# Edge counts by blocks of 16 targets instead of 32, and the one-hots of a block made in two operations

## The reference

```python
xn = _layernorm(x)
neigh = jax.ops.segment_sum(xn[src], dst, num_segments=1250)      # 40,000 edges
rst = (1.0 + eps[0]) * xn + neigh
gnn = relu(rst @ W1 + b1) @ W2 + b2 + xn
attn = relu((q * SCALE) @ k.T) @ v                                # 8 heads of 64, over all 1250 rows
x = x + gnn + (attn @ W_out.T + b_out)
x = x + experts(_layernorm(x))                                    # 16 experts, the 2 best of each row
```

## Time and profile before

| | us |
|---|---|
| median of 3 runs | 813.71 |
| the profiled execution | 813.19 |
| its span | 811.4 |
| lay-out of the edges, up to the first projections' end | 26.0 to 65.6 |
| projections with counts | 65.6 to 123.8 |
| V projection with counts and sums | 123.8 to 168.0 |
| attention with counts and sums | 168.0 to 439.7 |
| output, dense layers, routing and experts | 439.7 to 811.4 |

### The profile page before, as it was taken

The page is one execution under the profiler, slowest core; times in us unless marked ns, Lnnn a source line. Parts: engine busy times, 40 slices in busy tenths (PEclk is TensorE's granted clock), DMA queues, the critical chain, the costliest instruction groups (busy, mean ns, idle before and its releaser), DMA issues.

```text
span 811.4 us, 11860 instructions
## 1 busy us (share of the span) xinstructions
PE 722.5 (89%) x3591; PEld 438.2 (54%) x3592; DVE 441.4 (54%) x1350; ACT 221.3 (27%) x456; POOL 133.8 (16%) x191
## 2 busy tenths in 40 slices
PE   4878889999999999999999999999995899999900
PEld 2444444455555555555555457778882367667600
DVE  5945665358788787697742233343556333332324
ACT  2212211133232232232332033233341033434400
POOL 8945334000000000000000000020212000000054
PEclk9899999999999999999999999999997589999955
DMA  9530000060634706173376500010238564343367
GB/s 293 164 130 0 1 0 2 0 241 35 259 113 161 266 10 260 74 253 135 140 271 228 213 0 1 1 64 15 79 133 321 239 250 137 105 138 121 116 186 233
DMA packets 48769, 109.34 MB, mean 135 GB/s; under 512 B 6700, under 2 KB 6716, under 8 KB 46272
## 3 DMA queue, kind: packets, MB, share of 16 engines
q1 hardware_dynamic: 43936, 89.03, 30.5%
q0 software_dynamic: 3616, 11.17, 4.4%
q10 hardware_dynamic: 1152, 8.39, 2.6%
HBM read 44.79 MB, written 63.78 MB: 134 GB/s over the span
## 4 chain that ended last, share of the span: by engine, by line
PE 81%; DVE 9%; POOL 3%; issue 3%; DMA 3%; ACT 1%; SPq 0%; POOLq 0%; DVEq 0%
PE bank L1208 11%; PE bank L1191 10%; PE bank L1299 8%; PE bank L1245 7%; PE bank L1360 7%; PE bank L1090 7%; PE bank L1127 6%; PE bank L1373 6%; PE bank L1159 5%; PE bank L1170 4%; PE bank L1230 4%; POOL arena L598 2%; PE bank L1336 2%; DMA arena<-in_x 2%; PE bank L1342 2%
## 5 line engine op out<-in xcount | busy, mean ns | idle before, releaser
L843 DVE TENSOR_SCALAR arena<-iota,arena 125x128 f16<-125x128 f16 x392 | 113.2, 289 | 43.8 <-PE bank L1090 32.5
L845 DVE TENSOR_SCALAR arena<-iota,arena 125x320 f16<-125x320 f16 x392 | 120.3, 307 | 0.0
L674 ACT ACTIVATE arena<-bank 128x416 f32<-128x416 f32 (+1 forms) x120 | 62.2, 518 | 155.1 <-PE bank L1191 152.1
L873 DVE TENSOR_SCALAR arena<-bank 128x416 f32<-128x416 f32 (+1 forms) x120 | 69.0, 591 | 61.8 <-PE bank L1191 61.6
L1208 PE MATMUL bank<-arena 128*64 128x416 f32 (+1 forms) x480 | 97.2, 525 | 0.4 <-DVE arena L873 0.4
L1159 PE MATMUL bank<-arena 128*128 128x416 f32 (+1 forms) x192 | 81.8, 579 | 3.2 <-DMA arena<-in_wqkv 1.9
L1090 PE MATMUL bank<-arena 125*128 125x320 f16 x392 | 72.1, 302 | 8.6 <-DVE arena L845 8.4
L1299 PE MATMUL bank<-arena 128*128 128x384 f32 (+2 forms) x256 | 70.3, 430 | 0.0
L1360 PEld LDWEIGHTS bank<-arena 128*128 128x128 f32 x448 | 52.8, 197 | 17.1 <-issue 15.7
L1360 PE MATMUL bank<-arena 128*128 128x128 f32 x448 | 55.1, 283 | 6.3 <-issue 5.3
L1159 PEld LDWEIGHTS bank<-arena 128*128 128x128 f32 x192 | 40.3, 217 | 35.5 <-issue 33.0
(11 more groups left out here) (210 smaller groups left out, 1033.3 us busy)
## 6 DMA issues: line engine op xcount, KB each, us to landing
slots<-arena SPq DMA_DIRECT2D x6, 5376.0 KB, 17.1
slots<-arena SPq DMA_DIRECT2D x2, 5120.0 KB, 16.6
arena<-in_ew SPq DMA_DIRECT2D x8, 1024.0 KB, 11.3
arena<-in_ew ACTq DMA_DIRECT2D x8, 1024.0 KB, 14.3
arena<-slots SPq DMA_DIRECT2D x32, 256.0 KB, 2.7
slots<-arena SPq DMA_DIRECT2D x28, 256.0 KB, 2.0
arena<-in_gw SPq DMA_DIRECT2D x2, 2048.0 KB, 10.2
arena<-in_wqkv SPq DMA_DIRECT2D x3, 1024.0 KB, 15.7
```

The costliest lines, as they stand in the source:

```text
L674: act.activation(probs[0:kt, s % NPB, 0, 0:n], bank[2 * (s % 2)][0:kt, 0:n], ACT.Relu).then_inc(p0_ready, 1)
L843: dve.tensor_scalar(ring[:, at_slot:at_slot + P], iota16[0:CE, 0:P], window_cols[:, i % WBUF, 1, k:k + 1], None, ALU.is_equal)
L845: dve.tensor_scalar(ring[:, at_slot + P:at_slot + OHW], iota16[0:CE, :], window_cols[:, i % WBUF, 0, k:k + 1], None, ALU.is_equal).then_in ...
L873: dve.tensor_single_scalar(probs[0:kt, s % NPB, 1, 0:n], bank[2 * (s % 2) + 1][0:kt, 0:n], 0.0, op=ALU.max).then_inc(p1_ready, 1)
```

## The change

- `WD` is 16: blocks of 16 targets, 80 of them. A block is given 6 chunks (the 79th 2, the last 1), 471 products in all, each 160 columns wide.
- DVE makes all one-hots of a block in two operations, `tensor_tensor` with both operands broadcast: the ramp over the chunks, the chunk's number over the ramp. One is 125 x 6 x 128, one 125 x 6 x 160. Before, each chunk had two `tensor_scalar` operations. The ring holds 2 blocks, and `onehots_ready` counts blocks.
- Two blocks stand side by side in a bank (`window_at`), and ACT copies both at once. The swap of two pairs at a change of windows is gone.
- POOL makes columns for 80 blocks of 6 instead of 40 of 10, into 8 places, four blocks ahead instead of two windows.
- `EARLY` is 16 and `EVERY` 1.675, so a stretch of targets has the same turns as before. A block is made in the turn of its first chunk; its products stand in the turns they would have by the old rule.
- The marks have 80 entries where they had 40, and are turned by two transposes in place of one.

```diff
-WD = 32
+WD = 16
-RING = 8
-WBUF = 4
+RING = 2
+WBUF = 8
+RW = max(-(-EDGES * WD // (N * CE)) + 1, 1) * OHW
...
+        def window_at(w):
+            return bank[AW[w // 2 % 2]][:, w % 2 * WCOL:w % 2 * WCOL + WCOL]
...
-        PREP, FROM, EARLY = 4, 8, 8
-        EVERY = 3.35
+        PREP, FROM, EARLY = 4, 8, 16
+        EVERY = 1.675
...
-                dve_after[made].append(("pair", w, k))
-                if w % 2 == 0 and k == USUAL[w] - 1:
-                    held = ("pair", w, k)
-                elif w % 2 == 1 and k == 0:
-                    pe_after[used(made)] += [("pair", w, k), held]
-                    act_after[used(made) + 1].append(("window", w - 1))
-                else:
-                    pe_after[used(made)].append(("pair", w, k))
+                if k == 0:
+                    dve_after[made].append(("window", w))
+                pe_after[used(made)].append(("pair", w, k))
             if w % 2 == 1:
-                act_after[used(made) + 1].append(("window", w))
+                act_after[used(made) + 1].append(("windows", w // 2))
...
-                    pool.wait_ge(onehots_ready, FIRST[w - WBUF + 1])
+                    pool.wait_ge(onehots_ready, w - WBUF + 1)
-            for _, what, i in sorted([(start(max(w - 2, 0)), "cols", w) for w in range(NW)]
+            for _, what, i in sorted([(start(max(w - 4, 0)), "cols", w) for w in range(NW)]
...
-                        act.activation(a_t[:, g % 2, :, (i % WPG) * WD:(i % WPG + 1) * WD],
-                                       bank[AW[i % 2]][:, 0:WCOL].rearrange("p (b d) -> p b d", b=NT),
+                        act.activation(a_t[:, g % 2, :, c:c + 2 * WD].rearrange("p b (a d) -> p b a d", a=2),
+                                       bank[AW[i % 2]][:, 0:2 * WCOL].rearrange("p (a b d) -> p b a d", a=2, b=NT),
...
-                if what == "pair":
-                    if k == 0:
-                        dve.wait_ge(cols_ready, i + 1)
-                    q = FIRST[i] + k
-                    if q >= RING:
-                        dve.wait_ge(onehots_used, q - RING + 2)
-                    dve.tensor_scalar(ring[:, at_slot:at_slot + P], iota16[0:CE, 0:P],
-                                      window_cols[:, i % WBUF, 1, k:k + 1], None, ALU.is_equal)
-                    dve.tensor_scalar(ring[:, at_slot + P:at_slot + OHW], iota16[0:CE, :],
-                                      window_cols[:, i % WBUF, 0, k:k + 1], None,
-                                      ALU.is_equal).then_inc(onehots_ready, 1)
+                if what == "window":
+                    n = USUAL[i]
+                    dve.wait_ge(cols_ready, i + 1)
+                    if i >= RING:
+                        dve.wait_ge(onehots_used, FIRST[i - RING + 1])
+                    hot = ring[:, i % RING * RW:i % RING * RW + n * OHW].rearrange("p (k c) -> p k c", c=OHW)
+                    for c, of in ((slice(0, P), 1), (slice(P, OHW), 0)):
+                        width = c.stop - c.start
+                        ins = dve.tensor_tensor(
+                            hot[:, :, c], iota16[0:CE, 0:width].unsqueeze(1).to_broadcast([CE, n, width]),
+                            window_cols[:, i % WBUF, of, 0:n].unsqueeze(2).to_broadcast([CE, n, width]), ALU.is_equal)
+                    ins.then_inc(onehots_ready, 1)
...
-                if k == 0 and w >= 2:
-                    pe.wait_ge(window_saved, w - 1)
-                q = FIRST[w] + k
-                pe.wait_ge(onehots_ready, q + 1)
-                product(w, ring, (q % RING) * OHW, k == 0, k == USUAL[w] - 1).then_inc(onehots_used, 1)
+                if k == 0 and w % 2 == 0 and w >= 4:
+                    pe.wait_ge(window_saved, w // 2 - 1)
+                if k == 0:
+                    pe.wait_ge(onehots_ready, w + 1)
+                product(w, ring, w % RING * RW + k * OHW, k == 0, k == USUAL[w] - 1).then_inc(onehots_used, 1)
```

More of the change, by code:

```diff
@@ L47 @@
 WCOL = NT * WD
-RING = 8
-WBUF = 4
+RING = 2
+WBUF = 8
 OHW = P + WCOL
-USUAL = [-(-EDGES * min(WD, N - w * WD) // (N * CE)) + 1 for w in range(NW)]
+RW = max(-(-EDGES * WD // (N * CE)) + 1, 1) * OHW
+USUAL = [-(-EDGES * max(0, min(WD, N - w * WD)) // (N * CE)) + 1 for w in range(NW)]
 FIRST = [sum(USUAL[:w]) for w in range(NW + 1)]
@@ L128, in layer @@
         marks = at(A_T + 2400, [2, NW, CJ], parts=CP)
-        marks2 = at(A_T + 3700, [2 * NW], parts=CP)
-        val_f = at(A_T + 4400, [500], parts=CP)
-        ring = at(RINGB, [RING * OHW // 2], parts=CE).bitcast(f16)
+        marks2 = at(A_T + 5000, [2 * NW], parts=CP)
+        val_f = at(A_T + 5700, [500], parts=CP)
+        ring = at(RINGB, [RING * RW // 2], parts=CE).bitcast(f16)
         src_i, dst_i, hi_i, lo_i, win_i, off_i = (
@@ L135, in layer @@
         NCP = NC + max(USUAL)
-        window_cols = at(RINGB + RING * OHW * 2, [WBUF, 2, max(USUAL)], parts=CE)
+        window_cols = at(RINGB + RING * RW * 2, [WBUF, 2, max(USUAL)], parts=CE)
         val = at(VALB, [NCP], parts=CE)
@@ L211, in layer @@
         last5 = sb("last5", [CP, CJ])
-        mincol = sb("mincol", [CP, 1])
+        mincol = sb("mincol", [NW, 2])
         minrow = sb("minrow", [1, 2 * NW])
@@ L620, in graph @@
                 for what, i in act_after[turn]:
[L621 to L624, removed]
+                    if what == "windows":
+                        act.wait_ge(onehots_used, FIRST[2 * i + 2])
+                        g, c = 2 * i // WPG, 2 * i % WPG * WD
+                        if c == 0 and g >= 2:
                             act.wait_ge(neigh_ps, g - 1)
-                        act.activation(a_t[:, g % 2, :, (i % WPG) * WD:(i % WPG + 1) * WD],
-                                       bank[AW[i % 2]][:, 0:WCOL].rearrange("p (b d) -> p b d", b=NT),
+                        act.activation(a_t[:, g % 2, :, c:c + 2 * WD].rearrange("p b (a d) -> p b a d", a=2),
+                                       bank[AW[i % 2]][:, 0:2 * WCOL].rearrange("p (a b d) -> p b a d", a=2, b=NT),
                                        copy).then_inc(window_saved, 1)
@@ L776, in _ @@
             dve.wait_ge(consts_ready, 2)
-            dve.tensor_single_scalar(win_i, dst_i, 5, op=ALU.arith_shift_right)
+            dve.tensor_single_scalar(win_i, dst_i, 4, op=ALU.arith_shift_right)
             dve.tensor_single_scalar(off_i, dst_i, WD - 1, op=ALU.bitwise_and)
@@ L803, in _ @@
             dve.wait_ge(mins_ps, 1)
-            dve.tensor_reduce(mincol[:, :], bank[AW[0]][0:2 * NW, 0:CP], X, ALU.min).then_inc(mincol_ready, 1)
+            dve.tensor_reduce(mincol[:, :], bank[AW[0]][0:NW, 0:2 * CP].rearrange("w (a p) -> w a p", a=2), X,
+                              ALU.min).then_inc(mincol_ready, 1)
             dve.wait_ge(min_ps, 1)
@@ L811, in _ @@
             link(dve.tensor_tensor(minrow[:, NW:2 * NW], minrow[:, NW:2 * NW], minrow[:, 0:NW], ALU.subtract))
-            for of, usual in ((minrow[:, NW:2 * NW - 1], USUAL[0]), (minrow[:, 2 * NW - 1:2 * NW], USUAL[NW - 1])):
+            full = N // WD
+            for of, usual in ((minrow[:, NW:NW + full], USUAL[0]), (minrow[:, NW + full:NW + full + 1], USUAL[full]),
+                              (minrow[:, NW + full + 1:2 * NW], USUAL[NW - 1])):
                 last = dve.tensor_scalar(of, of, float(1 - usual), 0.0, ALU.add, ALU.max)
@@ L834, in _, with do @@
             dve.sem_inc(chunks_ready, 1)
[L835 to L847 removed]
+            def do(what, i):
+                if what == "window":
[10 more added lines that the diff above has]
+                    ins.then_inc(onehots_ready, 1)
                 else:
@@ L1070, in lay_out_edges @@
                     pe.wait_ge(marks_ready, 1)
-                    pe.transpose(bank[AW[0]][0:2 * NW, 0:CP], marks2, ident[0:CP, 0:CP]).then_inc(mins_ps, 1)
+                    for a in range(2):
+                        ins = pe.transpose(bank[AW[0]][0:NW, a * CP:(a + 1) * CP], marks2[:, a * NW:(a + 1) * NW],
+                                           ident[0:CP, 0:CP])
+                    ins.then_inc(mins_ps, 1)
                 elif part == 1:
                     pe.wait_ge(mincol_ready, 1)
-                    pe.transpose(bank[NB][0:1, 0:CP], mincol[:, :], ident[0:CP, 0:CP]).then_inc(min_ps, 1)
+                    for a in range(2):
+                        ins = pe.transpose(bank[NB][0:1, a * NW:(a + 1) * NW], mincol[:, a:a + 1], ident[0:NW, 0:NW])
+                    ins.then_inc(min_ps, 1)
                 elif part == 2:
@@ L1118, in neighbours @@
                 if t == 0:
-                    pe.wait_ge(window_saved, WPG * (g + 1))
+                    pe.wait_ge(window_saved, WPG // 2 * (g + 1))
                     if g:
```

2 lines of the change are left out of this document (1 added, 1 removed).

## The result

| | median us | runs from to | profiled execution | its span |
|---|---|---|---|---|
| before | 813.43 | 812.87 to 814.99 | 813.19 | 811.4 |
| after | 819.81 | 819.24 to 820.42 | | 817.5 |

The change makes the kernel slower: the ratio is 1.0073, with a 95% interval of 1.006 to 1.0086. The prediction was 801, with a range of 790 to 812, and was wrong in the sign too. Nearly all of the miss lies in one stage.

The account below looks back on a forecast made before the run. TensorE was taken to bound attention and the V stage, with stalls in projection. Gains of 20.3 - 12 + 1.7 + 4.6 - 0.8 - 0.9 = 12.9 us took 813.19 to 800.3, median 801; range 790 to 812.

Parts of the forecast that it names:

- Count products: TensorE, three stages: 160-column products 0.072 us apart against 0.138 for 320; gain 20.3 us, 16.3 of it in attention.
- A block's 1.93 us of DVE: DVE's two one-hot operations for a block take 1.93 us with waits, bounds 1.75 and 2.5; DVE is not relieved.
- Lumps in attention, 12 us: Attention: one-hots made in lumps delay ReLUs and counts, so TensorE stalls 12 us in all; the least trusted term.
- The slope of 4 us for ten per cent: Attention: stalls grow by 4 us if a block takes 10% longer, and fall by 4 if 10% less.
- First episode, +1.7: Projection stage, block 3 beside POOL's split: 2.2 us stall, lower clock in half the cases, instead of 4.6; gain 1.7.
- Second episode, +4.6: Projection stage, 23.9 us after the first episode: block 7 is ready before its first product is due; no stall, gain 4.6.
- First block, -0.8: Projection stage: TensorE's first count waits for a block of 1.93 us rather than a pair, behind POOL's columns; loss 0.8.
- edge lay-out, -0.9: Projection stage, TensorE's wait for the marks: sixteen operations of 80 instead of 40 elements and a larger reduction; loss 0.9.
- "Nothing changes place on TensorE": TensorE, all stages: its part of the change taken as 471 products instead of 392, with a gain of 20.3 us.
- rival 1: Lumps eat the gain: a block takes 2.5 us, attention 10 more than before, the rest 6 less; 817 us, chance 0.10.

Follow-up runs that it names:

- single pairs: Changed kernel with the spread looks, attention's one-hots made chunk by chunk, each pair by two scalar-per-partition operations with its own count: 793.99 us, again 792.97.
- the spread looks: Changed kernel, each tile's four sequencer checks for surplus chunks (register load and branch) placed ahead of source blocks 3, 5, 7, 9, not all before the last: 802.62 us.
- two looks: Changed kernel with one sequencer check for surplus chunks (register load and branch) per four blocks instead of two, so two per 128-target tile: 803.03 us.
- the kernel before with four looks: Kernel before, with a sequencer check for surplus chunks per window of 32 targets instead of per two, so four per 128-target tile: 829.77 us, ratio 1.0185.

## Why the prediction was wrong, step by step

- **Count products**: the spacing is right, the sum 1.3 us too high. Seven take 0.59 us until the values begin; less the 0.09 for the change of kind, that is 0.071 each, where the sum had 0.072. But where a neighbour sum follows, the last count product costs 0.03 us at either width: three of 320 columns take 0.31 us until the sum begins, which is two spacings of 0.138 and 0.03, and four of 160 take 0.25, three spacings and 0.03. At these 19 places the narrower product saves nothing of the 0.066. With single pairs, where hardly a wait is left, attention is 13.1 us shorter than before; 16.3 less 1.3 and less the 1.7 of waits is 13.3. Timelines of TensorE, two rows of after and two of before:

```profile
213.94 0.66 PE L1097 MATMUL bank<-arena 125*128 125x160 f16 x7
214.53 1.62 PE L1215 MATMUL bank<-arena 128*64 128x416 f32 x8
...
248.61 0.58 PE L1090 MATMUL bank<-arena 125*128 125x320 f16 x3
248.92 0.51 PE L1127 MATMUL bank<-xn_hi,a_t 128*128 128x512 f32 x1
```

- **A block's 1.93 us of DVE**: right, 1.94. It did not get slower beside POOL's small operations; those get longer beside it (the subtraction up to 1.03 us instead of 0.24), which costs nothing.
- **Lumps in attention, 12 us**: right in mechanism and near in size. With the spread looks the waits for DVE come to 10.2 us, and making pairs singly again gives back 9.9 and leaves waits of 1.7. The longest one, at 305.54, is that of block 53, with a residual sum behind it, as the prediction said (2.3 forecast, 1.78 + 0.35 measured). The slope of 4 us for ten per cent was 3.2 at most.
- **First episode, +1.7**: better. The wait is 1.68 instead of 2.2, and no lower clock stands behind it, so some +2.9. **Second episode, +4.6**: gone, as forecast.
- **First block, -0.8, and edge lay-out, -0.9**: right and half of it. The projection behind the first block starts at 68.64 (the second row below, of after) instead of 67.36. Of these 1.28 us 0.48 come from the edge lay-out, as DVE begins at 66.05 instead of 65.57, and 0.8 from the block. What the forecast did not have: the lower clock behind this first wait lasts longer. The eight projections there take 5.42 us until the next count product (68.64 to 74.06), where they took 4.49 (67.36 to 71.85), 0.9 more. That the projection stage came out 6.9 us better against 7.1 is partly luck: the episode gave 1.2 more and the lay-out 0.4, the clock took 0.9, and the rest I did not trace.

```profile
68.13 0.72 PE L1097 MATMUL bank<-arena 125*128 125x160 f16 x4 [4.27 <-DVE arena L846]
68.64 3.75 PE L1166 MATMUL bank<-arena 128*128 128x416 f32 x5
```

- **"Nothing changes place on TensorE"**, and the sum that rested on it: this is the step that failed. The prediction's section on TensorE's counts took its part of the change to be 471 products instead of 392. It counted matrix instructions and waits, and left out what the sequencer executes between them: twenty more looks, two more in each row of two. They cost 17.4 us of attention (285.90 against 268.50 with the same looks spread), where the sum had nothing. None of the rivals had it either; rival 1 (817) came near the time for a reason that doesn't hold, as a block takes 1.94 and not 2.5 us. The trace of before had what was needed: the load of L1103 took 0.30 us at some tiles and 0.90 at three, two looks took some 3 us there, with no wait behind them. How much is queued ahead of such a row can be counted in the timeline (3.3 us, above), and then a third look would not have fitted; there were two more.

With that one thing taken away, by two looks or by spread ones, the kernel takes 803.0 or 802.6 us against a forecast of 801, and attention 268.5 to 268.9 against 267 to 268.

## What to carry to other kernels

When a change makes a loop's unit smaller, go through everything that is done once per unit, on the sequencers too: register loads, branches and semaphore work count as no busy time, and are hidden only as long as enough is queued ahead of them. Ask how near the limit the existing cover is, above all where a large transfer runs beside it, since a step that is free at two in a row may cost 3 us at four. Where several such steps stand in a row, spreading them between pieces of work costs next to nothing, and it took the whole loss away here.

## What the runs showed of the hardware

- A register load by TensorE's sequencer from SBUF takes 0.30 us, and 0.87 to 0.95 in the changed kernel (up to 1.04 in the one with two looks) while a DMA of zeros at some 385 GB/s runs beside it; a whole look grows from 1.0 to 1.57 us. Moving the transfer alone brought it back to 0.30.
- 2.5 to 3 us without a matmul in the midst of a stage at full clock can be followed by 3 us or more at the lower clock: it was so behind all three long waits of the changed kernel (eight products took 3.06 us instead of 1.63), but behind one of three in the kernel before with four looks. A wait of 1.78 us at the same products was followed by it in one kernel and not in another. In attention of the changed kernel it cost 8.65 us of busy time on top of 10.5 of waiting, so a wait can cost more than its own length.
- DVE's comparison with both operands broadcast, 768 or 960 elements for each partition, costs nearly as much as six pairs with a scalar for each partition: 1.94 us against 2.0 for the same one-hots.
